# A two-layer transformer kernel: ScalarE takes negative parts, value evictions and second norms

## The reference, cut to what matters

```
xn = (x - mean) / sqrt(var + eps)
# layer 0 attention: linear, 16 heads of 16
qp, kp = elu(q) + 1, elu(k) + 1           # q, k, v = xn @ W.T + b
kv = kp.T @ v                              # per head
out = (qp @ kv) / (qp @ sum(kp) + 1e-6)
# layer 0 ffn: ternary weights, silu(up) * gate, down
# layer 1 attention: rotary, softmax over 1024 keys
# layer 1 ffn: Hadamard-rotated, silu(gate) * up, down
```

## Time and profile before

| | |
|---|---|
| median of 3 runs | 756.72 us (756.57 to 757.7) |
| the profiled execution | 757.94 us, of which the profile's span is 756.1 us |
| mean granted clock | 0.975 |
| PE busy | 702.5 us (93%) |
| DVE busy | 550.8 us (73%) |
| ACT busy | 419.2 us (55%) |
| POOL busy | 309.3 us (41%) |

### The profile page before, as it was taken

How to read it: one execution, slowest core, us unless ns; L and a number is a source line. 1 busy time by engine, 2 the same in 40 slices (tenths; PEclk the granted TensorE clock), 3 DMA queues, 4 the chain that set the end, 5 groups by cost and what they waited for, 6 DMA issues and landing times.

```text
span 756.1 us, 10955 instructions
## 1 busy us (share of the span) xinstructions
PE 702.5 (93%) x4186; PEld 440.5 (58%) x4186; DVE 550.8 (73%) x896; ACT 419.2 (55%) x560; POOL 309.3 (41%) x285
## 2 busy tenths in 40 slices
PE   4778898979988989999999998999999999999998
PEld 3556797968666778777667675333333333333445
DVE  4896766676677846677888887888888188888415
ACT  2242223424534533343232435999999899999883
POOL 1248766344845856244343541121233213422510
PEclk9898999998999999999999998999999999999999
DMA  6127101001104372251301110344434244432221
GB/s 254 56 84 264 56 2 56 1 1 57 55 1 148 119 262 84 84 196 57 103 11 57 56 57 18 130 145 134 145 89 156 92 164 153 137 110 90 89 92 56
DMA packets 25847, 74.13 MB, mean 98 GB/s; under 512 B 4620, under 2 KB 5996, under 8 KB 24964
## 3 DMA queue, kind: packets, MB, share of 16 engines
q1 hardware_dynamic: 21268, 65.37, 25.9%
q0 software_dynamic: 3808, 7.60, 3.4%
q10 hardware_dynamic: 720, 0.48, 0.2%
HBM read 54.54 MB, written 23.06 MB: 103 GB/s over the span
## 4 chain that ended last, share of the span: by engine, by line
PE 60%; POOL 2%; DVE 2%; ACT 1%; issue 1%; DMA 0%; SPq 0%; DVEq 0%; POOLq 0%; ACTq 0%
PE PS L1020 17%; PE PS L758 12%; PE PS L1006 12%; PE PS L764 8%; PE PS L989 6%; PE PS L979 4%; DVE mx L1321 1%; POOL sg L1613 1%; ACT P L1505 1%; POOL rot L1633 1%; POOL rot L1634 1%; DMA scr_k<-spl 0%; PE PS L995 0%; POOL hl L1604 0%; ACT spl L1487 0%
## 5 line engine op out<-in xcount | busy, mean ns | idle before, releaser
L1505 ACT ACTIVATE P<-PS 128x1024 f32<-128x1024 f32 x256 | 249.4, 1025 | 31.6 <-PE PS L1006 31.2
L1328 DVE TENSOR_REDUCE mx<-PS 128x1 f32<-128x512 f32 x300 | 189.2, 683 | 34.5 <-PE PS L989 32.8
L1321 DVE TENSOR_REDUCE mx<-PS 128x2 f32<-128x1024 f32 x106 | 124.8, 1221 | 37.3 <-PE PS L979 37.0
L1020 PE MATMUL PS<-P,VV 128*32 128x512 f32 x1024 | 137.4, 608 | 0.1
L1604 POOL TENSOR_TENSOR hl<-sg,hh 128x512 fp32r<-128x512 f32 x64 | 84.4, 1319 | 120.0 <-ACT hh L1475 67.4
L1006 PEld LDWEIGHTS PS<-QS,KS 64*128 64x128 f32 x512 | 49.0, 185 | 124.0 <-ACT P L1505 110.8
L1006 PE MATMUL PS<-QS,KS 64*128 64x512 f32 x512 | 117.7, 459 | 2.2 <-DVE mx L1321 1.8
L989 PE MATMUL PS<-KM,QM 64*128 64x512 f32 x300 | 82.3, 402 | 0.0
L1461 ACT ACTIVATE sg<-PS,cols 128x512 f32<-128x512 f32 x32 | 22.1, 690 | 81.9 <-PE PS L758 81.9
L1613 POOL TENSOR_TENSOR sg<-sg,us 128x512 f32<-128x512 f32 x32 | 42.1, 1315 | 37.4 <-ACT us L1470 37.4
L758 PE MATMUL PS<-XH,UGH 128*128 128x512 f32 x128 | 54.1, 422 | 1.6 <-ACT sg L1461 0.8
(11 more groups left out here) (208 smaller groups left out, 1406.2 us busy)
## 6 DMA issues: line engine op xcount, KB each, us to landing
QM<-scr_q SPq DMA_DIRECT2D x16, 512.0 KB, 4.3
KM<-scr_k SPq DMA_DIRECT2D x16, 512.0 KB, 5.2
QS<-scr_q SPq DMA_DIRECT2D x16, 512.0 KB, 4.4
KS<-scr_k SPq DMA_DIRECT2D x16, 512.0 KB, 5.2
scr_q<-spl SPq DMA_DIRECT2D x24, 256.0 KB, 3.4
scr_k<-spl SPq DMA_DIRECT2D x24, 256.0 KB, 3.5
scr_o<-OE POOLq DMA_DIRECT2D x14, 256.0 KB, 2.7
stg<-in_tern SPq DMA_DIRECT2D x3, 1024.0 KB, 4.8
```

Of the source, the lines that this page charges most:

```text
L1020: i = e.matmul(PS[32 * c:32 * c + 32, 7, :], v_head(8 * b + kt, 2 * j + c // 2), P[s % 4][:, chunk(c // 2 + 2 * (c % 2))], start=(kt == 0) ...
L1321: e.tensor_reduce(mx[p % 2][:, :, qt, half], PS[:, b:b + 2, :], AX.X, ALU.max).then_inc(q["mx"], 2)
L1328: e.tensor_reduce(mx[p % 2][:, h, qt, half:half + 1], bank[b], AX.X, ALU.max).then_inc(q["mx"], 1)
L1505: e.activation(P[s % 4][:, half * 1024:(half + 1) * 1024], PS[:, b:b + 2, :].rearrange("p b n -> p (b n)"), ACT.Exp).then_inc(q["ex"], 1)
```

## The change

It has six parts. (1) The value half of `kv_in` goes from DVE to ACT, as a copy without bias; `kv_sums` adds the value bias times the sum of the keys instead, before masking. (2) The minimum of the keys on POOL goes; ACT writes `relu(-zk)` into `ek` and takes `exp(-ek)`. Both stand in ACT's new `kv_sum`, which the list puts two tiles behind `kv_in` instead of one. (3) ACT also takes the negative part of the queries from the bank, `relu(-z - bias)`; DVE keeps the positive part and waits for ACT's to be done. (4) For norms 4 to 7 DVE computes -mean times reciprocal deviation (four columns), and ACT makes the four passes of 256 columns with scale and bias. (5) The four layer-1 `bias` pieces move from behind `ln_norm` to steps 4, 12, 20 and 28 of the first FFN chunk of layer 1. (6) `low_attn1` 0 is put one `prep_ug` earlier.

```diff
     def kv(tt):
         put("kv_in", tt, ps.next())
-        if tt % 8 > 0:
-            put("kv_sum", tt - 1)
+        if tt % 8 > 1:
+            put("kv_sum", tt - 2)
...
     def kv_end(b):
+        put("kv_sum", 8 * b + 6)
         put("kv_sum", 8 * b + 7)
...
         next(norm)
-        put("bias", 1, c)
...
-            if u == 1:
+            if u == 0:
                 put("low_attn1", 0)
...
+                if layer and c == 0 and k in (4, 12, 20, 28):
+                    put("bias", 1, k // 8)
                 yield
...
@@ DVE @@
             def ln_norm(n):
                 e.wait_ge(q["lnr"], n + 1)
-                if n == 6:
-                    e.wait_ge(q["pu"], 4)
-                if n == 7:
-                    e.wait_ge(q["lnb"], 14)
+                if n >= 4:
+                    e.scalar_tensor_tensor(nmr[i][:, :], mv[i][:, :, 0], -1.0, rstd[i][:, :], ALU.mult, ALU.mult).then_inc(q["lnm"], 1)
+                    return
...
+                e.tensor_scalar(MINUS_QB[:, :], cols[:, COLS["qb0"][0]:COLS["qb0"][0] + 2], -1.0, None, ALU.mult).then_inc(q["sus"], 1)
...
                 e.tensor_tensor(zk[j][:, :], bank[b][:, 0:256], BKV[:, 0:256], ALU.add).then_inc(q["kvz"], 1)
-                e.tensor_tensor(ve[j][:, :, 0:128], bank[b][:, 256:512].rearrange("p (g n) -> p g n", g=2),
-                                BKV[:, 256:512].rearrange("p (g n) -> p g n", g=2), ALU.add).then_inc(q["kvv"], 1)
...
                 for g in range(2):
-                    e.tensor_tensor(kvb[g][:, 0:128], bank[2][:, g * 129:g * 129 + 128], MASK[:, :], ALU.mult)
-                    i = e.tensor_scalar(kvb[g][:, 128:136], MASK[:, 0:128:16], bank[2][:, g * 129 + 128:g * 129 + 129], None, ALU.mult)
+                    total = bank[2][:, g * 129 + 128:g * 129 + 129]
+                    e.tensor_scalar(kvb[g][:, 128:136], MASK[:, 0:128:16], total, None, ALU.mult)
+                    e.scalar_tensor_tensor(kvb[g][:, 0:128], BKV[:, 256 + g * 128:384 + g * 128], total, bank[2][:, g * 129:g * 129 + 128],
+                                           ALU.mult, ALU.add).then_inc(q["kvb"], 1)
+                for g in range(2):
+                    e.wait_ge(q["kvb"], 2 * b + g + 1)
+                    i = e.tensor_tensor(kvb[g][:, 0:128], kvb[g][:, 0:128], MASK[:, :], ALU.mult)
                 i.then_inc(q["kvs"], 1)
...
             def q0(c, m, b):
-                e.wait_ge(q["qp"], i + 1)
-                if i >= 2:
-                    e.wait_ge(q["qg"], i - 1)
-                e.tensor_scalar(zs[m][:, :], bank[b], col("qb0", m), 0.0, ALU.add, ALU.min).then_inc(q["qn"], 1)
+                e.wait_ge(q["qn"], i + 1)
                 e.tensor_scalar(QP[:, m, chunk(c)], bank[b], col("qb0", m), 0.0, ALU.add, ALU.max).then_inc(q["qr"], 1)
...
@@ ACT @@
+            def ln_norm(n):
+                c, i = n % 4, n % 2
+                if n < 4:
+                    return
+                e.wait_ge(q["lnm"], n - 3)
+                if n == 6:
+                    e.wait_ge(q["pu"], 4)
+                if n == 7:
+                    e.wait_ge(q["lnb"], 14)
+                for t in range(4):
+                    e.activation(ln_buffer(n)[:, t, :], X[:, 4 * c + t, :], ACT.Identity, bias=nmr[i][:, t:t + 1], scale=rstd[i][:, t:t + 1]).then_inc(q["lnn"], 1)
...
             def kv_in(tt, b):
                 j = tt % 4
+                e.wait_ge(q["kvz"], tt + 1)
+                if tt >= 4:
+                    e.wait_ge(q["kvo"], tt - 3)
+                e.activation(ve[j][:, :, 0:128], bank[b][:, 256:512].rearrange("p (g n) -> p g n", g=2), ACT.Copy).then_inc(q["kvv"], 1)
+
+            def kv_sum(tt):
+                j = tt % 4
+                e.wait_ge(q["kvz"], tt + 1)
+                if tt >= 4:
+                    e.wait_ge(q["kvk"], tt - 3)
+                e.activation(ek[j][:, :], zk[j][:, :], ACT.Relu, scale=-1.0).then_inc(q["kvm"], 1)
                 e.wait_ge(q["kvm"], tt + 1)
-                e.activation(ek[j][:, :], ek[j][:, :], ACT.Exp).then_inc(q["kve"], 1)
+                e.activation(ek[j][:, :], ek[j][:, :], ACT.Exp, scale=-1.0).then_inc(q["kve"], 1)
 
             def q0(c, m, b):
-                e.wait_ge(q["qn"], 2 * c + m + 1)
-                e.activation(zs[m][:, :], zs[m][:, :], ACT.Exp).then_inc(q["qe"], 1)
+                i = 2 * c + m
+                e.wait_ge(q["qp"], i + 1)
+                if i == 0:
+                    e.wait_ge(q["sus"], 3)
+                if i >= 2:
+                    e.wait_ge(q["qg"], i - 1)
+                e.activation(zs[m][:, :], bank[b], ACT.Relu, bias=MINUS_QB[:, m:m + 1], scale=-1.0).then_inc(q["qn"], 1)
+                e.wait_ge(q["qn"], i + 1)
+                e.activation(zs[m][:, :], zs[m][:, :], ACT.Exp, scale=-1.0).then_inc(q["qe"], 1)
...
@@ POOL @@
-            def kv_in(tt, b):
-                j = tt % 4
-                e.wait_ge(q["kvz"], tt + 1)
-                if tt >= 4:
-                    e.wait_ge(q["kvk"], tt - 3)
-                e.tensor_scalar(ek[j][:, :], zk[j][:, :], 0.0, None, ALU.min).then_inc(q["kvm"], 1)
```

More of the change, by code:

```diff
@@ L29 @@
 SEMAPHORES = """
-init lns lnv lnd lnr lnn lnb lnh lnl bx fold w0h w0l sus
+init lns lnv lnd lnm lnr lnn lnb lnh lnl bx fold w0h w0l sus
 ta ts tc tl tp tt suh sgd
-kvp kvz kvv kvm kve kvk kvo kvs
+kvp kvz kvv kvm kve kvk kvo kvb kvs
 qp qn qr qe qg
@@ L458, in program @@
         mxc = [sb(f"mxc{i}", 27.8125 + i / 16, [128, 16]) for i in range(2)]
+        MINUS_QB = sb("MINUS_QB", 27.96875, [128, 2])
         MINUS_HALF = sb("MINUS_HALF", 27.9375, [128, 4])
@@ L503, in program @@
         mv = [sb(f"mv{i}", 207.5 + i / 32, [128, 4, 2]) for i in range(2)]
+        nmr = [sb(f"nmr{i}", 207.625 + i / 32, [128, 4]) for i in range(2)]
         rstd = [sb(f"rstd{i}", 207.5625 + i / 32, [128, 4]) for i in range(2)]
@@ L1527, in last @@
                     e.activation(LH[:, qs], OE[0][:, qs], ACT.Copy).then_inc(q["lh"], 1)
-            parts = {f.__name__: f for f in (start, ln_turn, w0h, tern_abs, kv_in, q0, att_t, prep_attn1, prep_down, prep_ug, gate, up,
+            parts = {f.__name__: f for f in (start, ln_norm, ln_turn, w0h, tern_abs, kv_in, kv_sum, q0, att_t, prep_attn1, prep_down, prep_ug, gate, up,
                                              hidden, qk_split, v, max_rows, scores, out, load_exp, last)}
@@ L1674, in low @@
                     e.wait_ge(q["fill"], 2)
-            parts = {f.__name__: f for f in (ln_stats, bias, fold, kv_in, q0, butterfly, low_attn1, difference, total, up, hidden, ones_v, qk_join, load_wl, out, recip, times, high, low)}
+            parts = {f.__name__: f for f in (ln_stats, bias, fold, q0, butterfly, low_attn1, difference, total, up, hidden, ones_v, qk_join, load_wl, out, recip, times, high, low)}
             for name, *args in order:
```

## The result

| | before | after |
|---|---|---|
| median of the runs of one comparison | 756.64 us (4 runs, 754.14 to 757.7) | 769.24 us (4 runs, 767.97 to 769.9) |
| ratio, 95% interval | | 1.0169 (1.0141 to 1.0198) |
| span of the profiled execution | 756.1 us | 767.9 us |
| mean granted clock | 0.975 | 0.971 |

The account below looks back on a forecast made before the run. The prediction took long stretches as bound by PE's own work, with only holes between to gain or lose. Terms 4.0 - 1.6 + 0.9 + 3.5 = +6.8 us on 757.94 gave 764.7, for the median 763.5 us, range 757.5 to 769.0.

Parts of the forecast that it names:

- to the last `kv_sum`: First batch's keys: DVE sheds evictions and minima but gains stalls and a wait on ACT's queue; +2.5 us.
- `kv_sums`: Before the first `att_n`: four DVE operations become six, with POOL in the way; +1.5 us, bounds 0.6 and 2.0.
- 61 to 165 us: Second batch: -1.1 us ahead of the hole at 80.87, -0.5 at 130.89, stalls between costing nothing; -1.6 us.
- second norms, net: Norms moved from DVE to ACT: +0.9 us at the first, +0.5 second, -0.5 third; sum +0.9, bounds -2.0 and +3.5.
- biases on POOL: Layer-1 additions: the first costs +1.2 us, the third +2.35 ahead of the rotations; +3.5, bounds +2.35 and +4.7.
- The stalls at `kv_sum`: Key tiles: DVE waits for ACT in twelve slots, 1.37 us each, where the eviction removed gave 0.33.
- The 1.9 us for the absolute values: End of first batch: ACT's third ternary matrix precedes the last keys' negative parts, so `kv_sum` 6 and 7 wait 1.9 us.
- The -0.5 us at 130.89: Last two keys of the second batch: ACT's tanh no longer stands behind POOL's minimum; -0.5 us.
- D: Rival: the hidden stalls between 82 and 125 us come out too, or both upper bounds; 769 to 773 us, chance 0.11.
- B: Rival: faster, DVE's relief decides in the early stage if ACT's exponential is done before `zk`; 754.2 us, chance 0.12.
- A: Rival: only the POOL part counts, key stalls overlap and the early stage ends even; 759.5 us, chance 0.20.
- E: Rival: negative part and exponential need different ACT tables, some 40 more loads; over 50 us more, chance 0.01.

Follow-up runs that it names:

- kv_only: The kernel before with parts 1 to 3 alone (keys, values, queries), norms and biases as they were: 762.94 us, ratio 1.0078.
- after_exp_first: The changed kernel, with ACT running the negative part and exponential of tile t-2 ahead of the value copy of t: 765.12 us.
- after_late_bias0: The changed kernel, with POOL's layer-0 bias additions put behind the first batch's keys and held until its `kv_sums` are done: 765.62 us.
- after_abs_late: The changed kernel, with ACT's absolute values of the third ternary matrix run at the first `kv_sums`, after the first batch's keys: 769.24 us.
- bias_only: The kernel before with part 5 alone, the layer-1 bias additions at steps 4, 12, 20 and 28: 760.09 us, ratio 1.0025.
- after_bias_back: The changed kernel without parts 5 and 6, layer-1 biases and `low_attn1` back at their old places: 764.56 us.
- all_mended: The same as kv_mended, with the second norms on ACT as well, as in the change: 751.36 us, ratio 0.9935.
- kv_mended: kv_only with ACT's exponentials first, its absolute values late and POOL's layer-0 biases held behind `kv_sums`: 751.33 us, ratio 0.9941 to the kernel before.

## Why the prediction was right or wrong

By its own sum, in the two profiled executions (+11.8 us):

| term | forecast | measured |
|---|---|---|
| to the last `kv_sum` | +2.5 | +4.5 (61.36 against 56.83); +3.0 in kv_only (59.81) |
| last `kv_out`, clock | as is | +0.3 (1.20 against 0.86 us) |
| `kv_sums` | +1.5, bounds 0.6 and 2.0 | +3.4 (5.76 against 2.40) |
| 61 to 165 us | -1.6 | -0.6 (7.62 at `att_n` 14 less 8.2) |
| second norms, net | +0.9 | +0.7 (8.33 less 7.62) |
| biases on POOL | +3.5 | +3.6 |

*The stalls at `kv_sum`* were right in cause, count and place: 1.20 us idle in each slot. By the forecast's own reckoning, from the start of `zk` less the 0.34 us after which DVE would be free, it is 44.41 - 42.78 - 0.34 = 1.29 us, for 1.37. after_exp_first shows the cause.

*The step that failed is the term for `kv_sums`, +1.5 us with an upper bound of 2.0, where +3.4 came.* It took the one 1.10 us at 59.18 as the price of a held operation. A held operation doesn't have a price of its own: it waits until the POOL operation in front ends, and POOL's were additions of 2.34 to 2.53 us, in a row. At 59.18 in the kernel before, POOL was not in a bias addition, as the forecast says, but in the shorter product behind one:

```profile
56.50 2.54 POOL L1552 TENSOR_TENSOR X<-X,OB 128x1024 f32<-128x1024 f32 x1
59.00 1.25 POOL L1571 TENSOR_TENSOR QP<-zs,QP 128x512 f32<-128x512 f32 x1
```

The operation ended at 60.28, the product at 60.25. The trace had the larger price, `kv_sum`'s 2227 ns and the 2.38 us of one addition, and the forecast quoted it without putting it into the term. Four of the six operations have all their tensors in SBUF (the column of sums aside), and three additions stood in POOL's queue. That would have given an upper bound of some 6 us: 0.6 for the operations, 7.1 for the additions, less the 1.6 that the hold cost before already (2.40 against 0.78 us at 131.61). after_late_bias0 takes the hold away, and `kv_sums` is back at 1.30 us. The whole stage, for which the forecast had +4.0 with an upper bound of 5.5, took +8.2, in kv_only +6.7, and the sign "the first L840 comes at 63 to 66 us" failed with 68.60. The Trainium skill (SBUF — State Buffer, SBUF: two separate sides) puts it as a lock for the whole instruction, where the other "fully blocks". The trace agrees: three ends of DVE's lie 0.02 to 0.15 us behind three ends of POOL's, and the operations with one of two tensors in PSUM pass in 0.34 us.

*The last `kv_sum`* has the same failure in it: the pair took 2.50 us where it takes 1.30 unheld, 1.2 us that the term didn't have. In kv_only the term measures +3.0, so without the hold +1.8 for the forecast 2.5: that the +3.0 came near the forecast is partly luck, a queue priced 0.7 too high and a hold left out. The other 1.5 us of the +4.5 are the clock from 40 to 50 us, and here "PE's clock I leave as it is" failed, though not by a rule: one execution of the same order has the spell and another hasn't. The 1.9 us for the absolute values came as 1.42 before the last maximum; after_abs_late shows that they were not what set the end.

*From 61 to 165 us:* `att_n` 3 regained 1.2 us, as forecast (1.1). The six stalls between 82 and 125 us cost nothing visible: from 90 to 130 us PE is busy 10.00 of each 10 us, and from `att_n` 3 to the hole's end at the last keys it is 49.7 us, 50.0 before (with the last two tiles behind it now, the last one only before). The -0.5 us at 130.89 failed: the hole is 2.87 us instead of 2.23, `att_n` 8 comes 7.65 us later where `att_n` 3 came 7.0 later. There too the pair waits for the exponentials, and `kv_sums` takes 1.30 us against 0.78 before (131.61 to 132.39).

*The norms* lost 1.1 us at the first place (forecast 0.9), 0.1 at the second (0.5), and gained 0.5 by the gate matmuls of layer 1 (0.5), where PE's hole of 1.57 us at 235.84 is gone. The four passes took 2.06 us, where the forecast took 1.85. The Trainium skill's rule (ScalarE: Activation LUTs, What ACT_TABLE_LOAD costs) had 2.1 for it, and the trace agrees with that: what the rows of before lacked was an operation with two pointer operands. No table load stands between the negative parts and the exponentials.

*The biases* are right on the chain: the first and the third addition are on it, the second and fourth not, the distance is +3.6, with the hole at 4.40 us for a forecast of over 5. bias_only shows them alone, after_bias_back takes them out again. "They leave POOL where PE did not wait on it" is wrong for the third norm, by the hole of 1.57 us; there the forecast's own -0.5, for the splits, names the cause.

*Rivals.* D was nearest in time (769 to 773), through "both upper bounds" only; its first half, hidden stalls between 82 and 125 us, did not happen. B named the condition on which DVE's relief would show, the exponential ready before the tile's `zk`. With that condition built in, and POOL out of the way, the first `att_n` comes 2.3 us earlier at the old clock (all_mended) and 4.3 at a better one (kv_mended), for B's 4.4. A fell with kv_only: 5.9 us for the key parts. E fell too: the trace after has three table loads, as the one before.

The 2.6 us by which the parts together cost more than their single sum are open in part. Some 1.6 of them fit the hole before 235.84, which part 4 and part 5 each remove when alone: after_bias_back, where the norms have removed it already, puts the biases at 4.7 us and not at 3.1. The rest lies within the intervals, and the clock spell adds doubt: it is 1.5 us in the one profile, but whether the four runs of the median had it isn't known.

## What to carry to other kernels

When work moves to another in-order engine, write out that engine's queue for one slot: a lag of two tiles hid nothing here, because the late tile's operations stood behind the early tile's copy, and putting two operations ahead of one took 16.1 us of waits down to 4.6. A DVE operation whose tensors all lie in SBUF (a column of scalars aside) should be priced by the POOL operation it may meet (here up to 2.5 us), for as many such operations as POOL has in a row, and not by one held sample of its own. A slower result need not mean that the idea is bad: with its order mended and POOL's free-floating additions held back, the same offload was 0.6% faster than the kernel before.

## What the runs showed of the hardware that was not expected

A `kvb` operation on 128x8 elements took 0.23 us alone and 2.12 us beside POOL's addition of 128x1024: the hold does not follow the size of the held operation. Three short DVE operations with all tensors in SBUF (the column of sums aside) each waited for a new POOL addition: between two of these DVE got one through, and then POOL's next held the following. The fourth passed (0.20 us behind the third) when POOL had no further addition.

PE's clock is a source of scatter that is easily read as an effect. From the third v matmul to the end, where no kernel of this study differs but for one or two additions on POOL, the profiled executions take either about 477.5 us (477.44 to 477.63 in four of them) or about 480.3 (480.18 to 480.45 in five), and five lie between. Stretches of lower granted clock fall differently: in the kernel before the 40 us behind that matmul are at 0.96, in kv_mended at 1.00. With the 1.5 us from 40 to 50 us, two profiled executions of one order of work can differ by some 4 us; the 29 runs of the kernel before in one comparison span 6.3. after_abs_late is the warning: against the one profile it seemed to gain 1.6 us, against another with the same granted clock nothing, and the median agrees with the latter.
